# Second-stage scan of a graph/SSM kernel: the scaled parts of token groups 0 and 1 are added to the accumulator by accumulating transfers of pairs, in place of GpSimd's additions

## The reference, cut to what matters

```python
h = jax.nn.relu(adj @ x @ gcn_w + gcn_b)
...
u = jax.nn.silu(xconv)
dbc = u @ w_xp
dt = jax.nn.softplus(dbc[:, :DT_RANK] @ w_dt + b_dt)
...
dA = jnp.exp(dt[:, :, None] * A[None])
dBu = dt[:, :, None] * B[:, None, :] * u[:, :, None]
def step(hst, inp):
    dAt, dBut, Ct = inp
    hst = dAt * hst + dBut
    return (hst, hst @ Ct)
_, ys = lax.scan(step, jnp.zeros((D_INNER, D_STATE), h.dtype), (dA, dBu, C))
y = ys + u * D_skip
y = y * jax.nn.silu(z)
return y @ w_out
```

## Time and profile before

| | |
|---|---|
| median of 3 runs | 2362.43 us (2361.44 to 2364.4) |
| profiled execution, first to last instruction (its span) | 2360.5 us; the profile gives no other time of that execution |
| PE busy | 2203.0 us, 93% |
| DVE busy | 1799.9 us, 76% |
| ACT busy | 1567.2 us, 66% |
| POOL busy | 1146.1 us, 49% |
| DMA, mean | 102 GB/s |

### The profile page before, as it was taken

How to read it: one execution, slowest core, us unless ns; L and a number is a source line. 1 busy time by engine, 2 the same in 40 slices (tenths; PEclk the granted TensorE clock), 3 DMA queues, 4 the chain that set the end, 5 groups by cost and what they waited for, 6 DMA issues and landing times.

```text
span 2360.5 us, 26229 instructions
## 1 busy us (share of the span) xinstructions
PE 2203.0 (93%) x8900; PEld 1388.7 (59%) x8900; DVE 1799.9 (76%) x2083; ACT 1567.2 (66%) x2541; POOL 1146.1 (49%) x926
## 2 busy tenths in 40 slices
PE   7998999999999999989999999999999987787998
PEld 4544545555555556546766666776766663444886
DVE  5666767777777765324989898999989898996665
ACT  5677686778686845425676867677676868774444
POOL 2101322222231313203988888888988888890000
PEclk9999999999999999999999999999999999798999
DMA  6243332333232323233423232333333221312121
GB/s 234 71 138 100 106 116 90 125 99 123 82 125 91 116 88 134 90 100 108 132 92 125 90 123 84 122 102 103 117 103 119 90 88 43 119 36 98 36 81 45
DMA packets 117111, 241.22 MB, mean 102 GB/s; under 512 B 8258, under 2 KB 65986, under 8 KB 116594
## 3 DMA queue, kind: packets, MB, share of 16 engines
q1 hardware_dynamic: 107906, 207.14, 26.8%
q0 software_dynamic: 8528, 31.36, 4.0%
q10 hardware_dynamic: 544, 1.05, 0.1%
HBM read 219.20 MB, written 20.32 MB: 101 GB/s over the span
## 4 chain that ended last, share of the span: by engine, by line
PE 65%; POOL 11%; ACT 10%; DVE 9%; issue 5%; DMA 0%; ACTq 0%; DVEq 0%; POOLq 0%
PE ps L684 13%; PE ps L726 10%; POOL dB L2301 7%; PE ps L970 5%; POOL acc L2283 2%; PE ps L848 2%; PE ps L822 2%; DVE h L1472 2%; PE ps L954 2%; PE ps L708 2%; ACT ps L1658 2%; ACT L1656 1%; POOL du L2297 1%; PE ps L754 1%; PE ps L752 1%
## 5 line engine op out<-in xcount | busy, mean ns | idle before, releaser
L1472 DVE TENSOR_TENSOR_SCAN h<-ps,hst,dB 128x512 f32<-128x512 f32 x512 | 637.2, 1271 | 64.5 <-ACT ps L1658 57.7
L2301 POOL TENSOR_TENSOR dB<-du,bc 128x512 f32<-128x512 f32 x512 | 648.9, 1290 | 61.2 <-DVE h L1472 58.4
L684 PE MATMUL ps<-wgt,msg 128*128 128x512 f32 x1024 | 488.4, 597 | 2.1 <-DVE xb L1180 2.1
L1658 ACT ACTIVATE ps<-dt,cols 128x512 f32<-128x512 f32 x512 | 351.0, 690 | 177.0 <-DVE h L1472 174.8
L726 PE MATMUL ps<-raw,msg 128*128 128x256 f32 x1792 | 443.1, 384 | 0.9 <-ACT hb L1658 0.9
L970 PEld LDWEIGHTS ps<-consts,h 128*128 128x128 f32 x2048 | 250.4, 144 | 221.2 <-issue 73.5
L970 PE MATMUL ps<-consts,h 128*128 128x128 f32 x2048 | 322.1, 283 | 61.0 <-DVE acc L1434 29.8
L726 PEld LDWEIGHTS ps<-raw,msg 128*128 128x128 f32 x1792 | 328.3, 193 | 76.2 <-issue 42.4
L684 PEld LDWEIGHTS ps<-wgt,msg 128*128 128x128 f32 x1024 | 189.6, 192 | 205.6 <-issue 203.9
L1658 ACT ACTIVATE wgt<-wgt 128x1024 f32<-128x1024 f32 x256 | 257.9, 1047 | 50.2 <-DVE wgt L1145 48.8
L2283 POOL TENSOR_TENSOR acc<-acc,part 128x512 f32<-128x512 f32 x174 | 226.2, 1300 | 61.3 <-ACT part L1658 60.2
(11 more groups left out here) (318 smaller groups left out, 3574.0 us busy)
## 6 DMA issues: line engine op xcount, KB each, us to landing
raw<-in_adjT SPq DMA_DIRECT2D x256, 512.0 KB, 3.6
bc<-tmp_bc SPq DMA_DIRECT2D x64, 512.0 KB, 4.7
E<-tmp_bc POOLq DMA_DIRECT2D x32, 512.0 KB, 4.2
xb<-in_xT POOLq DMA_DIRECT2D x8, 512.0 KB, 4.3
tmp_x<-xb POOLq DMA_DIRECT2D x8, 512.0 KB, 4.2
x<-tmp_x SPq DMA_DIRECT2D x8, 512.0 KB, 5.2
tmp_x<-x SPq DMA_DIRECT2D x8, 512.0 KB, 4.8
msg<-in_W SPq DMA_DIRECT2D x4, 1024.0 KB, 10.7
```

The lines of the kernel that those rows point to most:

```text
L684: x = e.matmul(P[d][:, :], msg[:, j, d * 128:(d + 1) * 128], wgt[g % NW][:, l, :], start=j == 0, stop=j == NJ - 1)
L1472: e.tensor_tensor_scan(hr[n % 3][:, m, :], PS[4 + k % 2].t[:, :], dBr[k % 4][:, :], hst[:, n % 16, m:m + 1], ALU.mult, ALU.add).then_inc(S ...
L1658: return e.activation(out, in_, func, bias=bias, scale=scale)
L2301: e.tensor_tensor(dBr[k % 4][:, :], du[:, m, :], bcr[i % 3][:, n % 2, :], ALU.mult).then_inc(S("dB"), 1)
```

## The change

`adder` says "moved" for s = 0 and s = 1 with n = 1 to 14 (where the units aren't already "tensor"), and "vector" for n = 15. ACT scales both groups' products into the two halves of one part buffer, now [128, 2, 512] and two of them, and POOL, after the second, issues one DMA from that buffer into `acc[:, 0:2, :]` with `accum_op=add`. Its landing is counted in the semaphore `d_acc`. Who waits on it: the next such DMA (for the one before it), ACT before it refills a part buffer (for the one two before), and DVE before its n = 15 addition (for n = 14). To make room, `th1` becomes the same memory as `x3`, with waits that keep the two uses apart; NPO becomes 19, so that the ACT sums of `post_b` come at its place in the table and not at the block's end.

```diff
-    if s == 0:
-        return "gpsimd" if n < 14 else "vector"
-    if s == 1:
-        return "gpsimd" if 2 <= n < 13 else "vector"
+    if s < 2:
+        return "moved" if n < 15 else "vector"
     return "vector"
...
+def moved_of(ib, n):
+    return [s for s in range(4) if adder(ib, n, s) == "moved"]
+MOVED = {x: i for i, x in enumerate((ib, n) for ib in range(NB) for n in range(16) if moved_of(ib, n))}
+def landed(ib, n):
+    return 16 * (MOVED[ib, n] + 1)
...
-        part = [sb(cB, f"part{i}", [128, 512]) for i in range(2)]
+        part = [sb(cB, f"part{i}", [128, 2, 512]) for i in range(2)]
...
-        th1 = sb(cB, "th1", [128, 2, TB])
+        th1 = x3
...
-        NP, NPA, NSA, NPB, NPO = 64, 55, 62, 71, 18
+        NP, NPA, NSA, NPB, NPO = 64, 55, 62, 71, 19
...
-        post_load = [1] * 8 + [0, 0] + mean_var
+        post_load = [1] * 8 + [0, 0] + mean_var + [0]
...
+                w.wait_ge(S("th1r"), 2 * min(ib + 2, NB))
                 e.dma_start(x3[:, :, :], t["x2"][:, :, blk]).then_inc(S("d_x3l"), 16)
...
-                        if last in HANDED:
-                            w.wait_ge(S("summed"), HANDED[last] + 1)
+                        if adder(*unit(last)) == "moved":
+                            w.wait_ge(S("d_acc"), landed(*unit(last)[:2]))
...
+                w.wait_ge(S("d_xn3"), 16 * (ib - 1))
+                w.wait_ge(S("sum"), 2 * (ib - 1))
...
-                        w.wait_ge(S("summed"), HANDED[j] - 1)
-                        act(part[HANDED[j] % 2][:, :], b.ps[:, :], ACT.Copy, scale=c).then_inc(b.evac, 1)
+                        w.wait_ge(S("d_acc"), landed(ib, n) - 32)
+                        act(part[MOVED[ib, n] % 2][:, s, :], b.ps[:, :], ACT.Copy, scale=c).then_inc(b.evac, 1)
...
-                e.tensor_tensor(acc[:, s, :], acc[:, s, :], part[HANDED[j] % 2][:, :], ALU.add).then_inc(S("summed"), 1)
+            def add(ib, n):
+                ss = moved_of(ib, n)
+                a, b = ss[0], ss[-1] + 1
+                for s in ss:
+                    made, last = hT_use(64 * ib + 4 * n + s), hT_use(64 * ib + 4 * n + s - 4)
+                    w.wait_ge(made.evac, made.n)
+                    if n > 1:
+                        w.wait_ge(S("d_acc"), landed(ib, n - 1))
+                    else:
+                        w.wait_ge(last.evac, last.n)
+                e.dma_start(acc[:, a:b, :], part[MOVED[ib, n] % 2][:, a:b, :], accum_op=ALU.add).then_inc(S("d_acc"), 16)
...
             for k in range(64 * NB + HAND):
-                if k - HAND in HANDED:
-                    add(k - HAND)
+                if k >= HAND:
+                    ib, n, s = unit(k - HAND)
+                    if (ib, n) in MOVED and s == moved_of(ib, n)[-1]:
+                        add(ib, n)
```

More of the change, by code:

```diff
@@ L48, in unit @@
     return j // 64, j % 64 // 4, j % 4
-HANDED = {j: i for i, j in enumerate(j for j in range(64 * NB) if adder(*unit(j)) == "gpsimd")}
+def moved_of(ib, n):
[3 more added lines that the diff above has]
+    return 16 * (MOVED[ib, n] + 1)
 SUMMED = {j: i for i, j in enumerate(j for j in range(64 * NB) if adder(*unit(j)) == "tensor")}
@@ L987, in gates @@
                             last, how = hT_use(64 * ib + 60 + s), adder(ib, 15, s)
-                            if how == "gpsimd":
-                                w.wait_ge(S("summed"), HANDED[64 * ib + 60 + s] + 1)
-                            elif how == "tensor":
+                            if how == "tensor":
                                 w.wait_ge(sum_use(ib, s).evac, sum_use(ib, s).n)
@@ L2274, in _ @@
             e.memset(hst[:, :, :], 0.0).then_inc(S("zero"), 1)
-            def add(j):
-                ib, n, s = unit(j)
-                made, last = hT_use(j), hT_use(j - 4)
-                w.wait_ge(made.evac, made.n)
-                if j - 4 in HANDED:
-                    w.wait_ge(S("summed"), HANDED[j - 4] + 1)
-                else:
-                    w.wait_ge(last.evac, last.n)
-                e.tensor_tensor(acc[:, s, :], acc[:, s, :], part[HANDED[j] % 2][:, :], ALU.add).then_inc(S("summed"), 1)
+            def add(ib, n):
[9 more added lines that the diff above has]
+                e.dma_start(acc[:, a:b, :], part[MOVED[ib, n] % 2][:, a:b, :], accum_op=ALU.add).then_inc(S("d_acc"), 16)
             for k in range(64 * NB + HAND):
-                if k - HAND in HANDED:
-                    add(k - HAND)
+                if k >= HAND:
+                    ib, n, s = unit(k - HAND)
+                    if (ib, n) in MOVED and s == moved_of(ib, n)[-1]:
+                        add(ib, n)
                 if k >= 64 * NB:
```

4 lines of the change are left out of this document (2 added, 2 removed).

## The result

The change makes the kernel slower: 2390.22 us median (2387.18 to 2394.74, 4 runs) against 2363.3 (2361.44 to 2364.4), ratio 1.012, 95% interval 1.0109 to 1.0132. The profiled execution has a span of 2385.4 us, 24.9 more than before. I had forecast 2374: slower, and by a new wait at each block's boundary, were right; the size, 12 us of the 27, was less than half. The step that failed first is the du that I had 1.94 us earlier at a boundary. The profiled execution is the fastest of the four; between the medians are 26.9 us.

The account below looks back on a forecast made before the run. No single engine bounds the scan: PE in mid-block, ACT around table loads, DVE with POOL behind near the boundary. 7 x (2.25 - 0.57) = +11.8 us on 2360.5, plus 1.9 for the median, gave 2374 us, range 2357 to 2398.

Parts of the forecast that it names:

- the du chain: Block boundary, POOL: only the second softplus addition holds du back, so first du and unit 3's dB come 1.94 us earlier.
- the credit for the first addition: First softplus addition on DVE, 1.85 us beside POOL work, falls to 1.28 with POOL's queue shorter: 0.57 us a block gained.
- L: Time from issue to landing of n = 14's transfer: taken as 5.5 us, bounds 3.1 and 8.4; a boundary costs L - 3.25.
- POOL's 174 additions mostly hidden: Away from the boundary, POOL's additions run in time nobody waits for; replacing them with transfers counts as nothing.
- The new wait at n = 15: Block boundary: DVE's n = 15 addition of group 0 waits for a landing, seven times, 3 to 5 us each.
- the 6.8 us that I drew from it: Landing time if an adding transfer runs at half a copy's rate: a boundary costs 3.55 us, the sum 21 instead of 12.
- The 0.65 us for n = 13 taken from DVE: Boundary: n = 13's group 1 addition leaves DVE directly ahead of the second softplus addition, bringing du 0.65 us earlier.
- ACT's added parts, the x3/th1 waits: nothing: ACT gets 202 parts for 174, 19 us over seven blocks, and waits on block-old events: both forecast to cost nothing.
- Rival 1: Boundary: the landing is hidden, L under 3.2; if wholly, -17.6 us, 2345 us; chance 0.17.
- Rival 3: Whole block: the chain of transfers sets the pace from L = 8.3; 2425 us at L = 9, 2516 at 10; chance 0.10.
- Rival 2: Boundary: no change, L between 3.2 and 4.5 as for plain transfers, 2358 to 2367 us; chance 0.17.

Follow-up runs that it names:

- n13_late1: Kernel after, with the transfer of n = 13 one unit later on POOL, behind du and dB of group 0: 2386.79 us.
- plain: Kernel after, with transfers that overwrite the accumulator instead of adding, so the sum lacks those additions: 2382.32 us.
- after_hold: Kernel after, with one more wait on POOL: a block's 60th dB waits for the next block's first softplus addition: 2393.93 us.
- pool_202: Kernel before with the new division of the sums but no transfers, POOL adding all 202 parts: 2380.35 us.
- split_before: Kernel after with the old division: transfers only where POOL added before, DVE adds the rest: 2378.09 us.
- before_n13v: Kernel before with n = 13 of group 0 added by DVE instead of ACT and POOL, no transfers: 2359.08 us against 2362.8, ratio 0.9987.
- n13_vector: Kernel after with n = 13 and 14 of groups 0 and 1 added by DVE, n = 12 the block's last transfer: 2379.02 us.

## Why the prediction was half right

The step of the sum that failed is the du chain. I had the first du 1.94 us earlier at a boundary, and with it the issue of the transfer on which everything behind waits; it came 0.24 us earlier against the softplus addition and 0.45 against the scan of unit 52. Two premises carried it: that only the second softplus addition holds du back, and that this addition comes 0.65 us earlier once DVE has less to do (1.22 with the credit for the first addition). The first is shown false by `n13_late1`, the second by the traces, where it comes 0.21 us earlier. The wait that I forecast is real, and L was too long by 1 us, which hid a part of the error.

- **POOL's 174 additions mostly hidden; nothing won by removing them.** Right. POOL fell to 1015.7 us, an issue to 0.88 us (0.61 to the next start), and mid-block states 7 to 12 changed by 1.4 us in total. But "nothing" was too much even there for states 3 to 6 (+5.6).
- **The new wait at n = 15 and its place.** Right: seven waits of 3.05 to 3.08 us, in the forecast's 3 to 5; moving the transfer by a unit moved the time by +7.2 and -4.5 us. Blocks 2 to 7 take 135.7 to 137.4 us instead of the 134 to 136 that I gave.
- **L = 5.5 us.** At the boundary it is 4.51, over all transfers 5.3. What I added for the extra read, 1.3 us, is near the 1.53 us between 4.51 and the 2.98 of `plain`; as a factor this is 1.51, and 5.3 / 3.4 = 1.56 over all. The Trainium skill gives half of a copy's rate for the adding transfers of a ReduceScatter among four ranks of a chip (Collectives: The Full Stack, "The bandwidth ceiling: the fold count and why AG ≠ RS ≠ AR"); for this single transfer within one core the 6.8 us that I drew from it do not fit this row. What I had too long was the plain copy, 4.2 us to memory against 2.98 within the chip.
- **The first du, 1.94 us earlier.** Failed. "POOL arrives early and only L1383 holds du back" overlooked the transfer of n = 13 in POOL's order, whose data come from ACT and not from POOL's own past. I had du 1.28 us after the softplus's start; it is 2.33 (2.57 before). `n13_late1` shows what I had assumed, 1.30. From du to the issue the chain is also 0.25 us longer, since the du behind an accumulating issue takes 1.57 us and not 1.29.
- **The 0.65 us for n = 13 taken from DVE, and 0.57 for the first softplus.** Failed: together they should have brought the second softplus 1.22 us earlier against the scan of unit 52; it came 0.21 earlier. "DVE is busy without a pause there" was the wrong premise; `after_hold` shows DVE waiting for ACT as soon as it is faster. The 0.57 was wrong in sign as well: the addition took 2.71 us, not 1.28.
- **ACT's added parts, the x3/th1 waits: nothing.** The waits cost nothing, right; the step that moves the sums costs 3.5 to 4.7 us, which I had not priced.

The sum again, for a boundary from unit 52 to unit 4: I had 1.68 us. Du and its chain 1.05 + 0.25 later, L 0.99 shorter, the second softplus 1.01 less early: 3.0, and the medians of the traces give 2.98 (35.44 against 32.46). Seven of them are 21 us, and the seven of the traces together 23.2, since the last one is longer. The rest of the profile is 5.6 us more in states 3 to 6, where the step lies, 1.8 less in the other states and 2.1 less outside the scan: 24.9. The error in L nearly cancelled the one in du, which was luck; the ones ahead of the second softplus, the last boundary and the step it did not cover.

Rival 1 did not come: the landing is not hidden. Rival 3 came at one place: of the 15.3 us that POOL waited for a landing, 9.2 are around the last boundary, where landings took 8.5 and 10.1 us, by its own bound of 8.3. At the other six the chain of transfers does not set the pace. Rival 2's L, 3.2 to 4.5, did come at the boundary, but not its time: with du and the softplus where they were, even L = 4.5 costs 21 us.

How the 27 us split depends on the order in which one counts. The new division costs 18 us when POOL adds (`pool_202`) and 12 when transfers do (after less `split_before`); the transfers cost 10 in the new division and 15 in the old, of which the step is 3.5 to 4.7. No run has the transfers without the step.

Open: what the four weight loads do to the landings at the last boundary; why the gain at a boundary is partly given back ahead of the next one (`before_n13v`, `n13_vector`), where the stretch from unit 52 to the second softplus is either about 17.3 or about 19.3 us from block to block, and by what wait the added step costs.
